# An RWKV block with mixture-of-experts layers: the order of ScalarE's queue in the last slot of each batch

## The reference

```
shifted = x moved by one token
key, value, rec = x*m + shifted*(1-m)            # three mixes, m per feature
k, v, r = key @ Wk, value @ Wv, sigmoid(rec @ Wr)
rwkv = decaying weighted mean of v with weights exp(k)   # a scan over the tokens
x = layernorm(x + (r * rwkv) @ Wo)
gate = softmax(x @ router.T), the two best of 8 experts kept
x = layernorm(x + sum over experts of gate * silu(x @ down.T) @ up.T)
```

## Time and profile before

| | |
|---|---|
| median of 3 runs | 472.66 us (472.56 to 473.25) |
| the profiled execution | 473.19 us |
| its span, first to last instruction | 471.4 us |
| TensorE matmul busy | 96% |
| VectorE busy | 88% |
| ScalarE busy | 75% |
| GpSimd busy | 64% |
| granted clock of TensorE, mean | 0.995 |

### The profile page before, as it was taken

How to read it: one execution, slowest core, us unless ns; L and a number is a source line. 1 busy time by engine, 2 the same in 40 slices (tenths; PEclk the granted TensorE clock), 3 DMA queues, 4 the chain that set the end, 5 groups by cost and what they waited for, 6 DMA issues and landing times. The chain is left out here.

```text
span 471.4 us, 6611 instructions
## 1 busy us (share of the span) xinstructions
PE 453.1 (96%) x1960; PEld 334.1 (71%) x1960; DVE 416.5 (88%) x621; ACT 354.8 (75%) x800; POOL 300.6 (64%) x287
## 2 busy tenths in 40 slices
PE   8999999999999999999999999999999999999993
PEld 3444656667888777877778777887778777878751
DVE  5989989799989979999899998999799997875866
ACT  1666765867787689886888778876898769768695
POOL 2454775589636987369846688279873696434335
PEclk9999999999999999999999999999999999999998
DMA  8603220033000042001320042100420012400015
GB/s 238 211 1 113 90 89 1 1 110 92 1 1 0 11 147 90 24 0 54 128 90 0 0 136 67 69 0 1 157 90 22 0 47 70 156 0 1 0 47 222
DMA packets 20100, 30.38 MB, mean 64 GB/s; under 512 B 2016, under 2 KB 7136, under 8 KB 20064
## 3 DMA queue, kind: packets, MB, share of 16 engines
q1 hardware_dynamic: 20064, 29.95, 19.5%
HBM read 21.56 MB, written 8.39 MB: 64 GB/s over the span
## 5 line engine op out<-in xcount | busy, mean ns | idle before, releaser
L566 ACT ACTIVATE PR<-PR 128x512 f32<-128x512 f32 x128 | 74.4, 581 | 30.6 <-DVE PR L864 16.2
L1156 POOL TENSOR_SCALAR NM<-SUM,RS 128x1 f32<-128x1 f32 x30 | 8.1, 269 | 106.5 <-ACT RS L566 106.5
L1150 POOL TENSOR_TENSOR DQ<-DEN,EX 128x512 f32<-128x512 f32 x32 | 41.8, 1306 | 21.1 <-DVE DEN L835 21.1
L889 DVE SCALAR_TENSOR_TENSOR KT<-D,VEC,XT 128x512 f32<-128x512 f32 x57 | 53.9, 982 | 1.2 <-POOL KL L1128 1.2
L317 PE MATMUL PK<-KH,WKH 128*128 128x512 f32 x112 | 48.2, 430 | 0.6 <-DVE NUM L852 0.6
L317 PE MATMUL PV<-VH,WVH 128*128 128x512 f32 x112 | 47.5, 425 | 0.0
L317 PE MATMUL PR<-RH,WRH 128*128 128x512 f32 x112 | 44.9, 401 | 1.9 <-DVE RW L876 1.3
L321 PE MATMUL PR<-RL,WRH 128*128 128x512 f32 x112 | 44.9, 401 | 1.4 <-POOL RL L1128 1.4
L835 DVE TENSOR_TENSOR_SCAN DEN<-PK,EX 128x512 f32<-128x512 f32 x32 | 39.0, 1219 | 6.5 <-ACT EX L566 4.7
L321 PE MATMUL PV<-VL,WVH 128*128 128x512 f32 x112 | 44.1, 394 | 0.5 <-POOL VL L1128 0.5
L321 PE MATMUL PK<-KL,WKH 128*128 128x512 f32 x112 | 44.0, 393 | 0.0
(11 more groups left out here) (249 smaller groups left out, 1266.8 us busy)
## 6 DMA issues: line engine op xcount, KB each, us to landing
XT<-in_xt SPq DMA_DIRECT2D x32, 256.0 KB, 3.5
XN<-in_x SPq DMA_DIRECT2D x28, 256.0 KB, 2.6
out<-XN SPq DMA_DIRECT2D x28, 256.0 KB, 2.0
X1T<-in_wo SPq DMA_DIRECT2D x1, 1024.0 KB, 5.2
XT<-in_x SPq DMA_DIRECT2D x4, 256.0 KB, 4.2
out<-XT SPq DMA_DIRECT2D x4, 256.0 KB, 2.4
X1T<-in_wk SPq DMA_DIRECT2D x2, 256.0 KB, 5.0
XN<-in_wv SPq DMA_DIRECT2D x2, 256.0 KB, 5.6
```

Of the source, the lines that this page charges most:

```text
L566: eng.activation(*a, **k).then_inc(q[s], 1)
L889: eng.scalar_tensor_tensor(out=full(b, which, c), in0=D[:, c, :], scalar=VEC[:, 2 + which, c:c + 1], in1=XT[:, c, 0:T], op0=ALU.mult, op1= ...
L1150: eng.tensor_tensor(DQ[:, :], DEN[:, 0:T], EX[:, 1, :], ALU.add).then_inc(q["e"], 1)
L1156: eng.tensor_scalar(NM1[:, col(t)], total, RS1[:, col(t)], scale, ALU.mult, ALU.mult)\
```

## The change

In the last slot of batches 2 to 6 (slots 11, 15, 19, 23 and 27), ScalarE's queue gets another order. Before: high halves 0 and 1 of the receptance mix, logarithm and factor, the three Relus of the next step, high halves 2 and 3, the three exponentials. After: high half 0, logarithm and factor, the three Relus, high halves 1 and 2, the exponentials, high half 3. Batch 1 keeps its order, and no instruction is added or dropped.

```diff
@@ -735,7 +735,7 @@
                 for t in past[:1]:
                     turned(t)
                 if j == 3 and b and batch(b + 1):
-                    highs(b + 1, 2, range(2))
+                    highs(b + 1, 2, range(1 if b > 1 else 2))
                 if s == C - 1 or 8 <= s < C * LAST:
                     log_g(s)
                     factor(s)
@@ -749,13 +749,15 @@
                     log_g(s)
                     factor(s)
                 if j == 3 and b and batch(b + 1):
-                    highs(b + 1, 2, range(2, C))
+                    highs(b + 1, 2, range(1, C - 1) if b > 1 else range(2, C))
                 for t in past[1:]:
                     turned(t)
                 if s < U - 1:
                     decay_exps(s + 1)
                 if s == 0:
                     high_weights(2)
+                if j == 3 and b > 1 and batch(b + 1):
+                    highs(b + 1, 2, range(C - 1, C))
                 for t in now[:1] if j == 3 and b < LAST else []:
                     halve(t + 1)
                 for t in past[:1]:
```

## The result

The changed kernel takes 466.67 us (466.59 to 466.72) against 472.96 us of the kernel before beside it: a ratio of 0.9868 (95% interval 0.985 to 0.9885), **6.3 us or 1.3% faster**. In a later comparison the two were 466.68 and 472.73 us (ratio 0.9876, 0.9857 to 0.9894).

What follows compares the result with a forecast made beforehand. A loop of ScalarE, GpSimd and VectorE was taken to set 55.0 us a batch. TensorE's 5.2 us of waits less 0.6 and 0.3 gave 4.3; 472.66 - 4.3 = 468.4 us, range 466.8 to 471.4.

Steps and rivals of the forecast that it cites:

- The loop: ScalarE, GpSimd and VectorE wait on each other in a closed loop without matmuls; it, not TensorE, sets 55.0 us.
- Parts (1) to (5): Slot 19: logarithm and factor leave ScalarE's busy stretch, Relus start 0.67 us earlier, product's halving (TH) 1.79; no new waits.
- Part (6): GpSimd, slot 19: its queue is next late, so normalising starts 1.26 us earlier and the loop becomes 53.7 us.
- 5.2 - 0.6 - 0.3 = 4.3 us: TensorE, slots 11 to 28: 5.2 us of waits, less 0.6 staying in slot 15 and 0.3 for wider starts.
- Each wait is followed by a start 0.1 us wider: TensorE: wider starts add 3 x 0.1 us for the low halves and 0.1 for the product.
- The 0.3 us that I left: TensorE: 0.3 us kept for wider starts after the low halves, since a tiny wait would bring them back.
- The 0.6 us of slot 15: TensorE, slot 15: of the 1.24 us wait for the product, 0.6 us stay.
- rival D: More gain: slot 15's draw won, 0.3 us not back, ScalarE wait after slot 28 gone; 467.1 us; chance 0.13.
- A: Rival: nothing gained, TensorE is 96% busy and DQ's wait swallows the gain; 472.2 or 472.7 us; chance 0.13.
- B: Rival: half a gain, port draw lost in other slots or another TensorE wait; 471.0 us; chance 0.14.
- C: Rival: slower, draw at mix 1 lost in slots 11, 19, 23 and 27; 474.7 us; chance 0.10.
- Decided within hundredths: VectorE and GpSimd at mix 1: who wins the shared port is decided within hundredths of a microsecond, anew every batch.

Runs made afterwards that it cites:

- with 1.11 us out: Changed kernel's order, but the Relus stay behind high 1 (logarithm and factor ahead of it, high 3 behind the exponentials): 468.09 us against 472.86 for the kernel before.
- with 1.0 out: Kernel before with only high 1 moved, behind the Relus: 469.4 us against 472.86.
- with 1.85 put back behind 0.5 of room: Changed kernel with three more 128 x 512 copies on ScalarE behind high 3: 472.41 us against 472.71 for the kernel before.
- the long memset: 128 x 256 memset on VectorE ahead of mix 1: kernel before 473.83 us, changed kernel 467.81, both against 472.76.
- the short one: 128 x 64 memset on VectorE ahead of mix 1: kernel before 472.7 us, changed kernel 466.46, both against 472.71.

## Why the prediction was wrong in size

**The loop** was right, and it is shown, not just argued. Four kernels put a known time into or out of ScalarE's stretch, and the batch follows: with 1.11 us out, 53.9 us (expected 53.9); with 1.0 out, 54.0 (54.0); with nothing out but high 3 moved, 55.0 (55.0); with 1.85 put back behind 0.5 of room, 55.05 (55.0 by what the copies really took; 54.7 to 54.9 had been expected for 1.6). One application in slot 11 gives 1.3 us once.

**Parts (1) to (5)** held to hundredths: 4.73 us from lead to TH where 4.71 was forecast, and no wait of GpSimd for a high half. **Part (6)** held in kind, with GpSimd next in line, and to a tenth in size: the normalising starts 278.24 - 269.96 = 8.28 us after the lead's end instead of 282.89 - 273.22 = 9.67, so 1.39 us earlier where 1.26 was forecast. The batch came out at 53.65 us; the forecast had 53.7 for the loop and 53.9 for TensorE.

**The sum is where it failed:** its step 5.2 - 0.6 - 0.3 = 4.3 us. It had TensorE's waits too small (0.1 us for the wide starts in each batch, nothing for the wait after slot 28) and kept two parts, 0.6 and 0.3 us, of which nothing stayed. To see what was really there, I took each matmul's start in both first traces, in program order, and looked where the difference grows: from -0.13 us ahead of slot 13 to -6.54 after slot 29.

- The four waits for the tile gave 2.3, the three for the low half 1.36, the product 1.24: 4.9 where 4.8 was summed. Right.
- **"Each wait is followed by a start 0.1 us wider"** was too small: 0.28 us a batch, not 0.1. Three starts ahead of each low-half wait are wide. In the kernel before, ahead of slot 20:

```profile
277.26 0.50 PE L317 MATMUL PR<-RH,WRH 128*128 128x512 f32 x1
277.60 0.39 PE L318 MATMUL PR<-RH,WRL 128*128 128x512 f32 x1
...
279.21 0.49 PE L321 MATMUL PR<-RL,WRH 128*128 128x512 f32 x1
279.54 0.40 PE L317 MATMUL PR<-RH,WRH 128*128 128x512 f32 x1
```

  Here 0.34 and 0.33 us lie between starts instead of 0.23, and the first of these matmuls itself starts 0.05 us late. No idle time is in the record; the operands had come only just before, the product at 277.21 and the third low half at 279.1. I take them for waits as well, too short for the list of waits; that the operand's lateness makes them is not shown by itself, but after the change all are at 0.23. Three batches and the 0.11 us behind the product of slot 15 make, with the small rest, 1.0 us instead of 0.4. This is also why TensorE's batch is 53.65 us and not 53.9.
- **The 0.3 us that I left** did not stay. All was won back.
- **The 0.6 us of slot 15** did not stay either. It rested on a lost port, and no slot of the changed kernel lost one. That is chance, and so is the 1.24 us wait before.
- **The wait after slot 28** The earlier trace rows gave 0.5 us. The prediction had put it into rival D only, although the other engines reach slot 28 with a lead like everywhere else.

4.3 + 0.6 + 0.3 + 0.6 + 0.5 = 6.3, and 0.1 for 4.9 instead of 4.8: the 6.4 measured between the two traces. The second traces of the two kernels, in which no port was lost, give 6.0 us from slot 13 on in the same way: 2.3 for the tile, 1.8 for four low halves, 0.5 after slot 28 and 1.4 in short waits before and after the low halves. So the miss isn't luck with the port in the main. This is rival D with the short waits that it did not have. Its time, 467.1, had been given a chance of 0.13 and set the range's low end with the spread of the runs alone.

**The rivals.** A (nothing, since TensorE is 96% busy) fell: the 96% hid a loop that is longer than TensorE's work. The rule of the Trainium skill (Perfetto Trace Analysis, "Identifying the Most-Contended Engine") is to optimize the engine with the highest occupancy first, with TensorE judged by other figures than its matmuls' busy time. ScalarE, at 75% against VectorE's 88%, is not the engine it names, and yet moving ScalarE's instructions gave 1.3%. B and C (the port lost more often) fell. "Decided within hundredths" was nearer the truth than its reason. VectorE won 77 of the 80 draws, with GpSimd's record ahead every time, and the three that it lost are those with the smallest lead of GpSimd in their group: 0.023 us, where the 59 won without a memset had 0.027 to 0.059, and 0.340 and 0.351 us, where the eight won with the long memset had 0.363 to 0.379. With the short one all ten were won at 0.151 to 0.183. The Trainium skill (SBUF — State Buffer, "SBUF: two separate sides") gives the port to whichever starts first. By the recorded starts that doesn't hold here. When GpSimd really asks for the port, no record tells, nor whether the lead decides the draw or is changed by it, and that part stays open.

## What to carry to other kernels

When the busiest engine waits a little in every period, follow those waits back until the chain meets itself: if it closes without that engine, the loop's length is the period, and the smallest thing that leaves the loop shortens every round. An in-order queue should not have work at its head whose operand comes late (high 1, waiting for mix 1) while work that is ready stands behind it (the logarithm), even on an engine with a quarter of its time free. And when adding up what there is to win, measure from start to start over the whole stretch and include starts that are only a tenth wider than usual; the list of waits shows 3.9 of the 6.4 us here. An empty list is no proof that nothing waits.

## What the hardware showed that I had not expected

- Where an operand was ready only just before (product at 277.21, matmul at 277.26), a start came 0.33 to 0.34 us after its predecessor instead of 0.23, without idle time in the record. Such starts made 0.28 us in each batch.
- GpSimd's normalising, recorded as started 0.15 us before VectorE's mix, took 1.27 us instead of 0.76 while the mix ran undisturbed. In all 77 cases of the 16 traces in which it was held up it ended 0.47 to 0.49 us after mix 1 did, whether its record was 0.03 or 0.38 us ahead. With the long memset either engine could be the one held up, with mixes of 3.34 or 4.38 us.
- In the changed kernel two bounds coincide to within 0.1 us a batch: TensorE without a wait in its list (53.65 of 53.65 us busy) and GpSimd without slack (0.2 us more on it, 0.2 us more a batch).
